# Cross attention on one core: row tiles over pairs of batches, fp16 score parts, context turned by DMA

## What is computed

```
q = (x @ Wq + bq).reshape(16, 100, 16, 64)         # 16 batches, 100 queries, 16 heads of 64
k = (ctx @ Wk + bk).reshape(16, 1444, 16, 64)      # 1444 keys of width 128
v = (ctx @ Wv + bv).reshape(16, 1444, 16, 64)
attn = softmax(einsum('bqhd,bkhd->bhqk', q, k) / 8)
out = einsum('bhqk,bkhd->bqhd', attn, v).reshape(16, 100, 1024) @ Wo + bo
y = layernorm(x + out) * gamma + beta               # x: 16 x 100 x 128
```

## Time and profile before

| | |
|---|---|
| time, median of 3 | 1006.57 us (1004.81 to 1007.61) |
| the profiled execution's own time | 1003.15 us |
| its span | 1001.3 us |
| mean granted TensorE clock | 0.982 |
| TensorE / VectorE / ScalarE / GpSimd busy | 95% / 89% / 83% / 31% |
| DMA engines' share in packets | 96.3% for the main queue |

### The profile page before, as it was taken

How to read it: one execution, slowest core, us unless ns; L and a number is a source line. 1 busy time by engine, 2 the same in 40 slices (tenths; PEclk the granted TensorE clock), 3 DMA queues, 4 the chain that set the end, 5 groups by cost and what they waited for, 6 DMA issues and landing times.

```text
span 1001.3 us, 26143 instructions
## 1 busy us (share of the span) xinstructions
PE 956.0 (95%) x10506; PEld 849.6 (85%) x10506; DVE 891.4 (89%) x1133; ACT 834.3 (83%) x1575; POOL 306.2 (31%) x287
## 2 busy tenths in 40 slices
PE   8799699999999999999999999999999999999996
PEld 7688588888988888888888888889888888888895
DVE  5789688999998999999998999989889899999883
ACT  3778689789898988989898898989889898988873
POOL 1405017632241504224050323415033241504210
PEclk8999799999999999999999999999999999999997
DMA  7488698999999999999999999999999999999997
GB/s 200 91 168 152 111 183 165 174 178 172 197 171 195 173 191 186 170 198 168 204 177 191 178 171 205 171 194 174 184 178 176 201 166 188 183 176 174 167 160 136
DMA packets 657858, 175.17 MB, mean 175 GB/s; under 512 B 628359, under 2 KB 656842, under 8 KB 657738
## 3 DMA queue, kind: packets, MB, share of 16 engines
q1 hardware_dynamic: 657306, 172.46, 96.3%
q10 hardware_dynamic: 432, 1.05, 0.4%
HBM read 15.87 MB, written 0.82 MB: 17 GB/s over the span
## 4 chain that ended last, share of the span: by engine, by line
PE 62%; DVE 13%; DMA 11%; SPq 6%; ACT 3%; issue 3%; POOL 1%; POOLq 0%; ACTq 0%
PE ps L516 15%; DMA pt_lo<-p_lo 11%; PE ps L521 10%; PE ps L498 9%; PE ps L499 9%; PE ps L500 9%; DVE nmax L693 5%; DVE p_lo L702 5%; SPq L340 5%; PE ps L414 4%; PE ps L406 3%; DVE ct_lo L641 1%; ACT p L854 1%; PE ps L398 1%; SPq L307 1%
## 5 line engine op out<-in xcount | busy, mean ns | idle before, releaser
L693 DVE TENSOR_REDUCE nmax<-ps 128x1 f32<-128x1446 f32 x208 | 344.9, 1658 | 57.7 <-PE ps L500 56.4
L702 DVE SCALAR_TENSOR_TENSOR p_lo<-p,rinv,p_hi 128x1444 f16<-128x1444 f32 x208 | 384.9, 1850 | 3.4 <-ACT p_hi L863 1.5
L863 ACT ACTIVATE p_hi<-p,rinv 128x1444 f16<-128x1444 f32 x208 | 312.9, 1504 | 0.0
L516 PEld LDWEIGHTS ps<-pt_hi,c_hl 128*128 128x128 f16 x4576 | 249.2, 98 | 55.6 <-issue 53.4
L516 PE MATMUL ps<-pt_hi,c_hl 128*128 128x128 f16 x4576 | 283.9, 218 | 5.0 <-issue 3.6
L498 PE MATMUL ps<-ct_hi,g_hi 128*128 128x482 f32 x624 | 257.5, 413 | 0.4 <-ACT p L854 0.4
L852 ACT ACTIVATE p<-ps,nmax 128x964 f32<-128x964 f32 x208 | 220.9, 1062 | 26.2 <-DVE nmax L693 25.9
L499 PE MATMUL ps<-ct_lo,g_hi 128*128 128x482 f32 x624 | 238.3, 382 | 0.0
L500 PE MATMUL ps<-ct_hi,g_lo 128*128 128x482 f32 x624 | 237.0, 380 | 0.0
L521 PE MATMUL ps<-pt_lo,c_hl 128*128 128x128 f16 x2288 | 159.0, 218 | 19.4 <-DMA pt_lo<-p_lo 18.9
L887 ACT ACTIVATE o_t<-ps,unscale 128x128 f32<-128x128 f32 (+1 forms) x208 | 75.5, 363 | 108.5 <-PE ps L521 106.6
(11 more groups left out here) (94 smaller groups left out, 826.3 us busy)
## 6 DMA issues: line engine op xcount, KB each, us to landing
c_raw<-in_ctx_dram SPq DMA_DIRECT2D x32, 256.0 KB
pt_hi<-p_hi SPq DMA_TRANSPOSE x208, 3.8
pt_lo<-p_lo SPq DMA_TRANSPOSE x208, 4.0
c_raw<-in_ctx_dram SPq DMA_DIRECT2D x16, 192.0 KB
c_raw<-in_ctx_dram SPq DMA_DIRECT2D x48, 18.0 KB
out_dram<-y SPq DMA_DIRECT2D x16, 50.0 KB
x_sb<-in_x_dram SPq DMA_DIRECT2D x1, 600.0 KB
o_t<-in_L_xattn_Wk_dram ACTq DMA_DIRECT2D x2, 256.0 KB, 3.8
```

Source lines behind the costliest of these rows:

```text
L516: pe.matmul(out_t, c_hl[:, par_c, i, part * D:(part + 1) * D], pt_hi[:, par, i, P - new:P], start=(i == 0 and part == 0), stop=False)
L693: dve.tensor_reduce(nmax[:, slot:slot + 1], ps[:, bank:bank + 3, 0:KEYW], AX.XY, ALU.max, negate=True).then_inc(s_nm, 1)
L702: dve.scalar_tensor_tensor(out=p_lo[:, par, 0:KL], in0=p32[:, buffer_of(slot), :], scalar=rinv[:, slot:slot + 1], in1=p_hi[:, par, 0:KL], ...
L863: act.activation(p_hi[:, par, 0:KL], p32[:, buffer_of(slot), :], ACT.Copy, scale=rinv[:, slot:slot + 1]).then_inc(s_hi, 1)
```

## The change

- A pair of batches is one run of 3200 rows in 25 row tiles (`IN_PAIR`), where it was 26. The tile in the middle (`MIXED`) holds the last 64 rows of one batch and the first 64 of the next: its scores are two matmuls of 64 rows for each product and range, in the two halves of the bank's partitions, and its weighing is done twice at 64 columns. A "window" of 12 tiles (even batches) or 13 tiles (odd batches) carries the jobs of a batch; `window(n)` gives the batch w and the place r.
- Scores are made from fp16 parts. The context is scaled and split first (`c_hi`, `c_lo`), and both parts are turned by DMA transposes on the SyncE queue at places 9 and 10 (`CT_HI_AT`, `CT_LO_AT`). TensorE's transposes of the context, and `ct_hi` and `ct_lo` out of a bank, are gone. The queries are scaled by `unscale`, which GpSimd multiplies into the bias and the factor (`query_scales`).
- The two padding columns of the third range are set to -1e30 once, and one exp covers 1446 columns. There are three `p32` buffers.
- The fp16 tensors are placed first in SBUF at multiples of 256 bytes, and each half of `p_hi` is 3072 bytes long, where it was 2888.
- GpSimd's order in a window is another: `query_scales`, all four query groups, `context_lo`, then `inverse_deviation`, `context_top` for the batch after the next, and `scale_rows`. Loads are at places 1 to 3, query projections at 1 to 4, projections through M at 6 to 9, `take_rows` at 10, the context's maxima at 8 to 10, and `context_scale` at 11.
- The prologue scales, splits and turns the first context by that path, makes the bias by small matmuls in place of a 1024-wide product, and runs the head products by two. The one-time splits `leave_lo` wait for `s_16h`, which ScalarE completes at tile 24, and they stand ahead of `query_scales` for batch 3.

```diff
-    NBLK = -(-ROWS // P)
-    NEW_ROWS = [P] * (NBLK - 1) + [ROWS - P * (NBLK - 1)]
+    WHOLE, HALF = divmod(ROWS, P)
+    IN_PAIR = 2 * WHOLE + 1
+    N = IN_PAIR * (B // 2)
+    G_AT = 1
+    G_AT_FIRST = 4
+    LOAD_AT = 1
+    STORE_AT = 2
+    CHI_AT = 5
+    FIN_AT = 6
+    CMAX_AT = 8
+    CT_HI_AT = 9
+    CT_LO_AT = 10
+    ROWS_AT = 10
+    NORM_AT = 11
+        sb("pad_to_256_bytes", [P, 32])
-        p_hi = sb("p_hi", [P, 2, KL], F16)
+        p_hi = sb("p_hi", [P, 2, KT * P], F16)
-        ct_hi = sb("ct_hi", [P, 2, KL], F32R)
+        ct_hi = sb("ct_hi", [P, 2, KT * P], F16)
+            for n in range(N + 2):                       # SyncE
+                if n >= 2:
+                    transpose_lo(n - 2)
+                if 1 <= n <= N:
+                    transpose_hi(n - 1)
...
+                if r == CT_HI_AT and w + 1 < B:
+                    transpose_context_hi(w + 1)
+                if r == CT_LO_AT and w + 1 < B:
+                    transpose_context_lo(w + 1)
+            def scores(n):                               # TensorE
...
+                for part in range(3):
+                    for k in range(3):
+                        a, e = KEYW * k, min(KEYW * k + KEYW, KL)
+                        for b, row, rows, at in segments(n):
...
+                            mm = pe.matmul(ps[at:at + rows, bank + k, 0:e - a], g, ct, start=(part == 0), stop=(part == 2))
+                act.activation(p32[:, n % P32S, :].rearrange("p (k w) -> p k w", w=KEYW), ps[:, bank:bank + 3, 0:KEYW],
+                               ACT.Exp, bias=nmax[:, i:i + 1], accum_out=psums[:, i:i + 1]).then_inc(s_exp, 1)
+            for w in range(B):                           # GpSimd
+                b = w + 1
+                if b < B:
+                    query_scales(b)
+                    for g in range(NG):
+                        split_queries(b, g)
+                    if w == 1:
+                        pool.wait_ge(s_axc, 1)
+                        pool.partition_all_reduce(ax_top[:, :], ax_max[:, :], P, RMAX).then_inc(s_axa, 1)
+                    context_lo(b)
...
+                if w > 0:
+                    inverse_deviation(w - 1)
+                if w + 2 < B:
+                    context_top(w + 2)
+                if w > 0:
+                    scale_rows(w - 1)
+                if w == 1:
+                    pool.wait_ge(s_16h, NG + NX)
+                    for i in range(2):
...
+                        leave_lo(2 * i, a_sb[:, heads, :], a16[:, heads], ax_scale[:, 0:1])
+                        leave_lo(2 * i + 1, xT[:, batches, :], x16[:, batches], ax_scale[:, 1:2])
```

More of the change, by code:

```diff
@@ L247, in every_other, with context_landed @@
             return slice(first, first + 2 * HG - 1, 2)
[L249 to L256, removed]
[L258 to L277 removed]
+        def context_landed(b):
+            return 16 * LOADS * (b // 2 + 1)
         def emptied(eng, k):
@@ L372, in _ @@
+            store(B - 2)
+            store(B - 1)
+            for par in range(2):
+                sp.wait_ge(s_out[par], 16 * (B // 2))
         @block.tensor
@@ new lines, in weigh @@
+            def weigh(n):
+                par = n % 2
+                for i, (b, row, rows, at) in enumerate(segments(n)):
+                    out_t = ps[:, O_BANK, at:at + rows]
+                    if n > 0:
+                        pe.wait_ge(s_ot, segments_before(n))
+                    if n == first_tile(b):
+                        pe.wait_ge(s_chl, b + 1)
+                    pe.wait_ge(s_th[par], halves(n))
+                    for t in range(KT - 1):
+                        for c in (c_hi, c_lo):
+                            pe.matmul(out_t, c[:, b % 2, t, :], pt_hi[:, par, t, at:at + rows],
+                                      start=(t == 0 and c is c_hi), stop=False)
+                    pe.wait_ge(s_tl[par], halves(n))
+                    for t in range(KT):
+                        c = c_hi[:, b % 2, t, :] if t < KT - 1 else c_tail[:, b % 2, :]
+                        mm = pe.matmul(out_t, c, pt_lo[:, par, t, at:at + rows], start=False, stop=(t == KT - 1))
+                    mm.then_inc(s_pv, 1)
@@ new lines, in copy_queries @@
+            def copy_queries(b, g, bank):
+                heads = slice(HG * g, HG * g + HG)
+                by = unscale[:, b % UNSCALES:b % UNSCALES + 1] if b < 3 else g_un_b[:, b % 2:b % 2 + 1]
+                return dve.scalar_tensor_tensor(
+                    out=g_raw[:, heads, :], in0=split(bank, HG, QL), scalar=by,
+                    in1=gb_b[:, b % 2, heads].unsqueeze(2).to_broadcast([P, HG, QL]), op0=ALU.mult, op1=ALU.add)
+            empty(0)
+            empty(2)
+            for g in range(NT):
+                context_max(0, g)
@@ L820, in _ @@
+            take_rows(B - 1)
+            norm_rows(B - 1)
         @block.scalar
@@ L990, in _ @@
+            context_top(0)
+            pool.wait_ge(s_gb, 1)
+            query_scales(0)
+            pool.wait_ge(s_clf, NT)
+            context_tail(0)
+            for g in range(1, NG):
+                cols = query_columns(g)
+                pool.wait_ge(s_part, g + 1)
+                pool.tensor_tensor(g_lo[:, 0, cols], query_group(g), g_hi[:, 0, cols], ALU.subtract).then_inc(s_gs, 1)
             pool.wait_ge(s_bvl, 16)
```

1121 lines of the change are left out of this document (532 added, 589 removed).

## The result

The kernel after takes 1030.77 us (median of 4 runs, 1024.00 to 1032.45), the kernel before in the same session 1005.69 us (4 runs, 1002.28 to 1007.61). The ratio is 1.024, 95% interval 1.018 to 1.030: slower by about 25 us, and the interval leaves open whether by more than 2%. The forecast was 965 us in a range of 915 to 1005; direction and range were both wrong. The profiled execution took 1032.44 us, its span is 1030.6 us.

A forecast was written before the change was run, and what follows sets the result against it. TensorE was taken as the bound; a steady batch falls from 58.4 to 50.7 + 2.9 + 1.5 + 0.5 = 55.6 us. Span 1001.3 - 34 - 8 + 3 - 2 = 960, so 965 us, range 915 to 1005.

The forecast's parts named there:

- Context by transfer: Two context transposes more per batch in SyncE's queue, replacing TensorE's: charged 0.5 us a batch, bounds 0 and 3.
- fp16 scores: TensorE's score matmuls at 482 columns: 205 ns each as fp16, nine in 1.85 us for 2.04.
- VectorE's 50.7 us a batch: VectorE's work per steady batch after the change, with half a tile and the `ct_lo` copies gone.
- TensorE's 52.8: TensorE's work in us per steady batch after the change, from 105.7 us a pair.
- 2.0 us for `c_top`: VectorE's wait at place 11 for GpSimd's reduction, 2.0 us every batch.
- The second wait: VectorE's wait at place 1 for GpSimd's query scales: 1.8 us after a twelve-tile window, hidden after a thirteen-tile one.
- The waits that come once: Early windows: 12.5 us for the low parts behind `leave_lo`, and VectorE's wait for `ax_top`, entered as +8.5.
- Prologue: Start to the first maximum: the first context's path with two transfers adds 3 us, bounds 0 and 8.
- First three batches: From the first maximum to that of window 3: 192 us for 199.8, so -8.
- SyncE's queue as the bound: Rival, chance 0.13: transposes' issues fill SyncE's queue, deciding from 1.9 us per issue; at 2.1 us, 1029 us.
- The halves in turn: Rival, chance 0.20: the mixed tile's two score halves run one after the other, 15 us more: 980 us.
- The free run: Rival, chance 0.27: VectorE and TensorE run free, waits and imbalance are absorbed, a batch takes TensorE's 52.8 us: 930 us.

The follow-up runs named there:

- e1: The kernel after with the two context transposes issued one place earlier in a window (8 and 9 for 9 and 10): 995.59 us, ratio 0.989.
- e4: The kernel after without the context's turning transfers of batches 2 to 15, their scores using the first two batches' context: 998.33 us, ratio 0.992.
- e3: The kernel after with the context transposes one place earlier and context_scale moved from place 11 to place 0 of the following window: 990.58 us, ratio 0.984.
- e9: e3 with the pad 32 bytes a partition longer, so the turning transfers' buffers start off 256-byte boundaries: 1024.37 us, ratio 1.017.
- e10: The edits of e3, e5 and e6 together, plus each context loaded in six pieces of two tiles instead of three of four: 930.84 us, ratio 0.927.
- e6: e3 with the query projections and their copies at places 2 to 5 instead of 1 to 4 from window 2 on: 966.54 us, ratio 0.959.
- e5: e3 with parts_scale at row tile 19 for 16, batch 3's query projections in fp32 and GpSimd's low halves made in two pieces: 969.27 us, ratio 0.963.
- run 24: Not a run's label: in "cost the run 24 us (e7)" the run is e3, and 24 us is the time e7 took off it.
- e7: e3 without the context loads of batches 4 to 15, computing with the four batches that are there: 966.22 us, ratio 0.960.
- e11: The edits of e3, e5 and e6 together, with context loads of batches 2 to 15 issued from ScalarE's queue instead of SyncE's: 939.24 us, ratio 0.934.

## Why the prediction was wrong

**The step that failed: "Context by transfer ... So I charge 0.5 us a batch".** It cost 35 us in all (e1), 28.0 of it in the twelve batches (719.8 to 691.8 us), that is 2.3 us a batch, near the upper bound of 3. The two transfers' load was not the cause (e4). The slack was reckoned for `pt_lo`: what does the extra issue do to the next tile's parts? The question that decided was when the context's own transfers come up in the queue, and the prediction put no term on it. SyncE comes to `ct_lo`, at its place 10, only when TensorE has finished the weighing of place 11, since the `pt_hi` ahead waits for a buffer that TensorE's weighing frees. In a twelve-tile window place 10 is followed by only one more place, so `ct_lo` goes out when it is already wanted. This was at hand: the same wait is the largest of SyncE's in the trace before (`SPq L289 <- PE ps L521: 95.0, 106, 3.3`: us, times, longest).

**What was left out: the loads.** The sum treated every landing as hidden. In e3, with the turns in time, the twelve batches still take 688.6 us; without loads they take 667.3, and the prediction had 667. That agreement is in part luck: with the buffers off their boundaries (e9) the same batches take 711.1 us, so the new layout gives 22.5 us of it, for which the sum had no term, and the wait for the query scales takes more than was summed (below). The prediction had the row (a DMA share above 1.0 in the steady part) and used it only as evidence for a rival. The kernel before has the same loads beside its transfers, but TensorE as its bound, so that more of the delay may have been hidden. That is argued, not shown: no run of the kernel before without loads was made.

**What was left out on the other side: the layout.** Alignment is worth 34 us on e3 and 15 us on the kernel before. The prediction noticed the boundaries and gave them no term. On the kernel after itself it wasn't measured; without it the change would presumably have been slower still.

**What was right.**
- fp16 scores: 205 ns predicted. A tile's nine matmuls run in about 1.84 us. VectorE's 50.7 us a batch was measured as 607.39/12 = 50.6; TensorE's 52.8 as 54.8, with the stretches at the lower clock in it. In e10 it is 638.39/12 = 53.2.
- GpSimd: 2.0 us for `c_top` was 2.4. The second wait (1.8 us after twelve-tile windows) was there only once the turn was early, and then 2.5 us a batch (32.3/13, in e3) where 0.9 was summed; moving the queries one place took 24 us (e6).
- The waits that come once, 12.5 and 8.5 us, were 12.9 and 8.1, and e5 took both away for 21 us. Prologue: +3 was +3.9. The end was 4.2 us shorter than predicted.
- First three batches: 20.6 us too short. Moving the turns gave 9 of them back (203.5 in e1). The rest was not taken apart.

**The rivals.** SyncE's queue as the bound had a chance of 0.13 and 1029 us. The number fits by luck and the mechanism does not: an issue takes 1.38 to 1.42 us in the median, far from the 1.9 from which it was to decide, and the queue is not full. It is late. (Its 8.4 us for loads and stores is too high as well: its own prices give 6.0 for the twelve loads, and a store takes 0.49 in the trace after; the 1.9 stays.) The halves in turn did not happen. The free run did not either. That e10 ends at 931 us, near its 930, is another sum: its twelve batches take 654.7 us where the free run has 12 x 52.8 = 634, and its start is shorter by the one-time waits that e5 removed. The range ended at 1005 because no case had two transfer effects at once: the late turn alone (+28 over twelve batches) gives some 993, with the loads (+21) it is past the end.

The runs lead from 1030.8 to 990.6 us by both moves of e3 (40 us), to 943 by the one-time waits and the queries' place (48), to 931 by smaller loads (12). The 66 us between forecast and measurement are not closed by this: the late turn is 35 of them, the loads 24 as measured on e3, and the layout's gain on the kernel after, of the other sign, was not measured.

## What to carry to other kernels

When a transfer is put into an in-order queue, find when that queue really reaches the place, from the issue times of its neighbours in the trace, and compare that with when the consumer starts; the place in the program is not the time. Ask above all what the transfer ahead of it waits for: here it was the consumer itself. If a rewritten kernel does less work on every engine and is slower, read the waits before giving the rewrite up: here two constants moved by one turned +2.4% into -1.1%, and four edits more into -7.3%. Start the buffers of turning transfers on 256-byte boundaries (34 and 15 us in the two kernels here), and try loads in smaller pieces beside them (12 us).

## What the hardware showed that was not expected

- 32 bytes of offset make the turning transfers' packets 11% slower (21.8 to 24.1 ns) and lengthen the issue on SyncE from 1.46 to 1.66 us; that is worth 34 us of 990.
- Loads of 256 KB cost the run 24 us (e7), with TensorE's waits for `pt_lo` 29.6 us where they are 10.5 without; the same bytes in smaller pieces cost 12 us less (e10), the same loads from ScalarE's queue 4 us less (e11).
- Behind each of the eight waits of 1.9 to 3.6 us at a mixed tile TensorE has a granted clock of 0.50 to 0.67 for the next 3.6 us, so a wait of TensorE costs more than it lasts: at 0.59 about 1.5 us more, an estimate from 3.6 x (1 - 0.59).
- Around `c_top` GpSimd stands twice: 79.1/13 = 6.1 us ahead of the reduction, and 93.0/13 = 7.2 us behind it, ahead of its next instruction (`zg`). The Trainium skill, "GPSIMD Engine Reference", 2.1 Instruction dispatch, names about 6 us for the first call of a freshly loaded kernel; the trace agrees with that for the first of the two in its length; that code is loaded there each time no run shows. Whoever puts urgent work behind such a reduction pays the second one: in e3 VectorE waited 32.3 us for it, and one place later 9.5.
